# An attention layer with two layer norms, on one core: new orders for the first three rounds and the last five pairs, and the last two tiles' output bias added by TensorE

## The reference, cut to what matters

```
xn  = layernorm(x)                        # x is 8 x 2048 tokens of 512
Q,K,V = xn Wq + bq, xn Wk + bk, xn Wv + bv    # each token: 16 heads of 32
P   = softmax over k of (Q[q] . K[k]) / sqrt(32)   # per token, q and k over the 16 heads
o   = P V, laid out as (head, token, 32) and read back as (token, 512)
y   = o Wo + bo
x1  = x + layernorm(y)                    # "A": statistics of y
z   = layernorm(layernorm(x1)) * ln_g + ln_b   # "B": statistics of x1, both norms at once
out = x1 + layernorm(z)                   # "C": statistics of z
```

## Time and profile before

| | us |
|---|---|
| median of three runs | 1566.44 |
| the profiled execution | 1567.45 |
| its span, first to last instruction | 1565.7 |
| TensorE busy | 1528.8 (98%) |
| VectorE busy | 1371.3 (88%) |
| GpSimd busy | 1356.3 (87%) |
| ScalarE busy | 839.7 (54%) |

### The profile page before, as it was taken

The page is one execution under the profiler, slowest core; times in us unless marked ns, Lnnn a source line. Parts: engine busy times, 40 slices in busy tenths (PEclk is TensorE's granted clock), DMA queues, the critical chain, the costliest instruction groups (busy, mean ns, idle before and its releaser), DMA issues.

```text
span 1565.7 us, 59257 instructions
## 1 busy us (share of the span) xinstructions
PE 1528.8 (98%) x22566; PEld 773.4 (49%) x22566; DVE 1371.3 (88%) x2476; ACT 839.7 (54%) x1754; POOL 1356.3 (87%) x1422
## 2 busy tenths in 40 slices
PE   7999999999999999999999999999999999999993
PEld 3445455455554554554554554554554554554541
DVE  7788988988988988988988889888889888888888
ACT  5445465465465565555554554554554554554654
POOL 3668988988988988988988989989989989889867
PEclk9999999999999999999999999999999999999997
DMA  6776766766766766766767767767767767767652
GB/s 235 196 173 162 215 171 191 212 167 195 212 165 198 211 168 198 210 166 202 206 166 206 203 166 208 201 167 210 199 166 212 196 168 213 193 169 214 163 138 95
DMA packets 388651, 293.71 MB, mean 188 GB/s; under 512 B 296854, under 2 KB 296854, under 8 KB 388380
## 3 DMA queue, kind: packets, MB, share of 16 engines
q1 hardware_dynamic: 345936, 223.54, 53.8%
q10 hardware_dynamic: 42444, 66.37, 13.6%
HBM read 155.46 MB, written 67.24 MB: 142 GB/s over the span
## 4 chain that ended last, share of the span: by engine, by line
PE 92%; DVE 3%; POOL 2%; DMA 1%; ACT 1%; issue 1%; SPq 0%; ACTq 0%; POOLq 0%; DVEq 0%
PE ps_k L1299 7%; PE ps_q L1299 7%; PE ps_v L1299 7%; PE ps_v L1300 7%; PE ps_y L1402 7%; PE ps_q L1300 7%; PE ps_k L1300 7%; PE ps_q L1302 7%; PE ps_y L1405 7%; PE ps_y L1401 7%; PE ps_k L1302 7%; PE ps_v L1302 7%; PE ps_s L1357 6%; PE ps_o L1379 5%; DMA x_t<-in_xt 0%
## 5 line engine op out<-in xcount | busy, mean ns | idle before, releaser
L1099 ACT ACTIVATE q_sb<-ps_q,qk_back 128x512 f32<-128x512 f32 x127 | 87.2, 687 | 411.3 <-PE ps_q L1302 400.4
L474 POOL TENSOR_TENSOR o_sb<-o_sb,x 128x512 f32<-128x512 f32 x122 | 153.6, 1280 | 90.6 <-ACT o_sb L1058 90.5
L444 POOL TENSOR_TENSOR x_t<-x_t,mr_row 128x512 f32<-128x512 f32 x126 | 194.4, 1543 | 19.9 <-DMA mr_row<-x_d 10.2
L451 POOL TENSOR_TENSOR x_t<-x_t,mr_row 128x512 f32<-128x512 f32 x126 | 194.8, 1546 | 0.5
L1401 PE MATMUL ps_y<-wo_hi,oT_hi 128*128 128x512 f16 x500 | 190.5, 381 | 0.0
L1402 PE MATMUL ps_y<-wo_lo,oT_hi 128*128 128x512 f16 x500 | 190.4, 381 | 0.0
L1299 PE MATMUL ps_k<-wk_hi,xT_hi 128*128 128x512 f16 x496 | 188.6, 380 | 0.0
L1299 PE MATMUL ps_v<-wv_hi,xT_hi 128*128 128x512 f16 x496 | 188.2, 379 | 0.0
L1300 PE MATMUL ps_v<-wv_lo,xT_hi 128*128 128x512 f16 x496 | 188.2, 379 | 0.0
L1299 PE MATMUL ps_q<-wq_hi,xT_hi 128*128 128x512 f16 x496 | 188.0, 379 | 0.1
L1300 PE MATMUL ps_k<-wk_lo,xT_hi 128*128 128x512 f16 x496 | 188.0, 379 | 0.0
(11 more groups left out here) (226 smaller groups left out, 3355.1 us busy)
## 6 DMA issues: line engine op xcount, KB each, us to landing
x_in<-in_xa SPq DMA_DIRECT2D x64, 512.0 KB, 6.4
x_t<-in_xt SPq DMA_DIRECT2D x64, 512.0 KB, 8.4
k_bd<-kT SPq DMA_DIRECT2D x512, 64.0 KB, 3.3
v_d<-v_tok ACTq DMA_DIRECT2D x128, 256.0 KB, 2.5
v_key<-v_d SPq DMA_DIRECT2D x128, 256.0 KB, 4.3
res<-in_xr SPq DMA_DIRECT2D x64, 512.0 KB, 5.7
p_bd<-pT ACTq DMA_DIRECT2D x500, 64.0 KB, 2.7
out<-o_sb SPq DMA_DIRECT2D x62, 512.0 KB, 7.3
```

The costliest lines, as they stand in the source:

```text
L444: nc.gpsimd.tensor_tensor(x_t[v % 2][:, j, :, :], x_t[v % 2][:, j, :, :], mr_row[v % 2][:, :, 0, j].unsqueeze(1).to_broadcast([P, EC, P]), ...
L451: nc.gpsimd.tensor_tensor(x_t[v % 2][:, j, :, :], x_t[v % 2][:, j, :, :], mr_row[v % 2][:, :, 1, j].unsqueeze(1).to_broadcast([P, EC, P]), ...
L474: nc.gpsimd.tensor_tensor(o_sb[:, v % 2, j, :], o_sb[:, v % 2, j, :], x1[:, v % 3, j, :], ALU.add).then_inc(out_done, 1)
```

## The change

It reorders the hand-written start and end of every list, and gives the last two tiles another way to get their bias.

* Start. `spread("v")` has another bank (`ps_o`) and waits no more for the evened keys' weight. DVE makes the first `xT_lo` ahead of `scale("k")`, evens out the values' weight later, and turns the first probabilities ahead of `scale("o")`; both `low("o")` go ahead of the loop. In `project` the low-by-high products come ahead of the high-by-low ones for tiles 0 and 1. ACT issues both first `probs_half_out` ahead of `v_in(2)`. SP has `next_x(4)`, `load_r(0)`, then `values_back(0)`, `keys_out(2)`, `values_back(1)`; `rows_load(3)` now stands behind `values_back(2)` and `values_back(3)`; `load_r(1)` a round later. `spare(14)` is `spare(16)`.
* End. PE runs `mixed(124)` ahead of `scores(126)` and `output(123)` ahead of `values(127)`. The lists of DVE, ACT, POOL and SP have other orders from pair 59 on.
* Bias. DVE makes `y_fore`, the product of the two weights' scales, and `y_eps`; ACT makes `bo_fore`, the bias times `y_fore`. PE writes it into the banks of tiles 126 and 127 with a one-row f32 matmul (`bias`) behind `mixed(126)`, and `output` adds to it. DVE's `end_sums("A")` and ACT's `end_turn("A")` then read the bank itself, so `y_in(126)` and `y_in(127)` are gone; `y_eps` scales the layer norm's epsilon to match.

The core of the diff:

```diff
@@ PE
-            pe.wait_ge(w_even, 2)
             spread("v")
...
-            spare(14)
+            spare(16)
             values(1)
...
             output(NT - 6)
+            mixed(NT - 4)
             scores(NT - 2)
             scores(NT - 1)
-            mixed(NT - 4)
             mixed(NT - 3)
+            output(NT - 5)
             values(NT - 1)
-            output(NT - 5)
             output(NT - 4)
             output(NT - 3)
             mixed(NT - 2)
+            bias(END + 2)
+            bias(END + 3)
             mixed(NT - 1)
...
+            def bias(t):
+                if t == END + 2:
+                    pe.wait_ge(bo_fore_done, 1)
+                    pe.wait_ge(y_done, END)
+                else:
+                    pe.wait_ge(vtok_done, NT)
+                nc.tensor.matmul(y_bank.get(t, ps_y[:, :]), ones[:, :], bo_fore[:, :], start=True, stop=False, skip_group_check=True)
@@ SP
             keys_out(1)
+            next_x(4)
+            sp.wait_ge(w_split, 4)
+            load_r(0)
             values_back(0)
+            keys_out(2)
             values_back(1)
             rows_of(2)
-            keys_out(2)
+            next_xt(3)
             probs_half_out(0)
             probs_half_out(1)
             keys_out(3)
-            next_xt(3)
-            rows_of(3)
-            sp.wait_ge(w_split, 4)
+            rows_store(3)
...
                 values_back(b - 2)
                 if p == 2:
-                    next_x(4)
-                    load_r(0)
+                    rows_load(3)
+                if p == 3:
                     load_r(1)
@@ DVE
+            dve.wait_ge(xhi_done, 1)
+            nc.vector.tensor_tensor(xT_lo[0][:, :, :], x_t[0][:, 0, :, :], xT_hi[0][:, :, :], ALU.subtract
+                                    ).then_inc(first_low, 1)
             scale("k")
...
             less_top(NT - 4)
+            z_stat(NV - 5, 0)
             less_top(NT - 3)
             weigh(NT - 4)
+            weigh(NT - 3)
+            z_stat(NV - 5, 1)
+            p_turn(NT - 4)
+            moments("C", NV - 5)
             k_turn(NT - 2)
-            p_turn(NT - 4)
-            z_stats(NV - 5)
-            weigh(NT - 3)
             x1_stats(NV - 4)
+            o_low(NT - 6)
+            p_turn(NT - 3)
+            o_low(NT - 5)
+            out_add(NV - 5, 0)
+            k_turn(NT - 1)
             q_turn(NT - 2)
-            out_add(NV - 5, 0)
+            z_add(NV - 4, 0)
+            q_turn(NT - 1)
...
             end_z_lean(END)
+            end_sums("A", END + 3)
             end_z_out(END)
-            end_sums("C", END)
-            y_in(END + 2)
-            end_sums("A", END + 2)
-            y_in(END + 3)
@@ ACT
             probs_half_out(0)
+            probs_half_out(1)
             v_in(2)
-            probs_half_out(1)
+            cast("o", 0, wo_hi)
             q_in(3)
+            cast("o", 1, wo_hi)
             x_high(4)
@@ POOL
             out_add(NV - 3, 0)
             out_add(NV - 3, 1)
+            end_root_of("B", END + 3, 1.0 + EPS, EPS * EPS)
+            end_out_add(END)
+            end_out_add(END + 1)
             end_root_of("C", END + 2)
```

More of the change, by code:

```diff
@@ L63, in fused @@
         y_back = sb("y_back", [P, 1])
+        y_fore = sb("y_fore", [P, 1])
+        y_eps = sb("y_eps", [P, 1])
+        bo_fore = sb("bo_fore", [1, E])
         x_in = [sb(f"x_in{i}", [P, 2, E]) for i in range(2)]
@@ L397, in _ @@
             values_back(NT - 3)
+            store(NV - 6)
+            keys_out(NT - 2)
+            probs_half_out(NT - 4)
+            keys_out(NT - 1)
+            probs_half_out(NT - 3)
             sp.wait_ge(x1_done, 2 * (NV - 4))
             load_r(NV - 3)
-            store(NV - 6)
-            keys_out(NT - 2)
+            values_back(NT - 2)
+            store(NV - 5)
+            store(NV - 4)
             sp.wait_ge(x1_done, 2 * (NV - 3))
             load_r(NV - 2)
[L404 to L409, removed]
             probs_half_out(NT - 2)
@@ L414, in _ @@
             load_r(NV - 1)
+            store(NV - 3)
+            end_store(END)
             end_store(END + 1)
-            end_store(END)
-            store(NV - 3)
             end_store(END + 2)
@@ L913, in _ @@
             low("v", 0, wv_hi, wv_lo)
+            low("v", 1, wv_hi, wv_lo)
             k_turn(1)
-            low("v", 1, wv_hi, wv_lo)
             q_turn(1)
@@ L920, in _ @@
             less_top(1)
+            weigh(0)
+            weigh(1)
+            p_turn(0)
+            q_turn(2)
+            p_turn(1)
+            k_turn(3)
             scale("o")
             product_scale(y_back, "v", "o", 1.0, y_scale_done)
[L923 to L928, removed]
             x_moments(3)
             q_turn(3)
+            low("o", 0, wo_hi, wo_lo)
+            low("o", 1, wo_hi, wo_lo)
             for p in range(2, NV - 1):
@@ L963, in _ @@
                     z_scale(v)
+            dve.wait_ge(w_scaled, 8)
+            nc.vector.scalar_tensor_tensor(y_fore[:, :], scale_of("v"), 1.0, scale_of("o"), ALU.mult, ALU.mult).then_inc(y_fore_done, 1)
+            dve.wait_ge(y_fore_done, 1)
+            nc.vector.scalar_tensor_tensor(y_eps[:, :], y_fore[:, :], EPS, y_fore[:, :], ALU.mult, ALU.mult).then_inc(y_fore_done, 1)
             y_in(NT - 7)
@@ L967, in _ @@
             less_top(NT - 4)
+            z_stat(NV - 5, 0)
             less_top(NT - 3)
             weigh(NT - 4)
+            weigh(NT - 3)
+            z_stat(NV - 5, 1)
+            p_turn(NT - 4)
+            moments("C", NV - 5)
             k_turn(NT - 2)
-            p_turn(NT - 4)
-            z_stats(NV - 5)
-            weigh(NT - 3)
             x1_stats(NV - 4)
-            q_turn(NT - 2)
-            out_add(NV - 5, 0)
-            out_add(NV - 5, 1)
[L978 to L985, removed]
+            o_low(NT - 6)
[3 more added lines that the diff above has]
+            k_turn(NT - 1)
+            q_turn(NT - 2)
+            z_add(NV - 4, 0)
+            q_turn(NT - 1)
+            z_stat(NV - 4, 0)
+            z_add(NV - 4, 1)
+            z_stat(NV - 4, 1)
+            out_add(NV - 5, 1)
+            moments("C", NV - 4)
+            y_in(NT - 6)
             less_top(NT - 2)
-            y_in(NT - 6)
+            less_top(NT - 1)
             y_stats(NT - 6)
-            less_top(NT - 1)
             weigh(NT - 2)
             o_low(END)
-            o_low(END + 1)
+            y_in(NT - 5)
             p_turn(NT - 2)
-            y_in(NT - 5)
             y_stats(NT - 5)
@@ L997, in _ @@
             y_in(END)
+            o_low(END + 1)
+            p_turn(NT - 1)
             end_sums("A", END)
-            p_turn(NT - 1)
             end_moments("A", END)
@@ L1173, in end_turn @@
                 act.wait_ge(end_shift[i], turn)
+                if k == "A" and t >= END + 2:
+                    act.wait_ge(y_ready, t + 1)
+                    act.wait_ge(out_done, 2 * (t // 2 - 3) + t % 2 + 1)
                 if k == "C" and t < END + 2:
@@ L1253, in _ @@
                 x_high(b + 2)
+            act.wait_ge(b_loaded, 3 * DMA)
+            act.wait_ge(y_fore_done, 1)
+            nc.scalar.activation(bo_fore[:, :], bo_row[0:1, :], ACT.Copy, scale=y_fore[0:1, 0:1]).then_inc(bo_fore_done, 1)
             o_high(NT - 6)
```

127 lines of the change are left out of this document (65 added, 62 removed).

## The result

The changed kernel took 1571.68 us (median of six runs, 1570.17 to 1574.16), the kernel before 1567.03 in six runs beside it (1565.5 to 1568.93). The ratio is 1.0029, with an interval of 1.0019 to 1.0039: slower, by 4.5 us, where 7.3 us faster were forecast. The profiled execution took 1570.17 us, the least of the six, and spans 1568.4 (before: 1567.45 and 1565.7).

What follows compares the result with a forecast made beforehand. TensorE, busy 1179.95 of 1180 us in the loop, was taken as the bound, leaving only start and end to win. Start 2.7, end 3.1 and behind the last matmul 1.5 made 7.3: 1566.44 to 1559.1 us, range 1555.5 to 1563.8.

Steps and rivals of the forecast that it cites:

- Start, up to the third tile: From the kernel's start to keys(2): reordered lists bring it 1.75 us sooner, between 0.6 and 3.8.
- Start, to the loop: From keys(2) to the loop: the 1.0 us p_bd wait goes, start total 2.7 us; a later rows_load(3) is made up.
- rival 3: In the loop: shifted instruction supply leaves TensorE gaps each round; at 0.2 us a round 1571.3 us; chance 0.06.
- Loop: The steady rounds between start and end: same instructions, so nothing won or lost.
- End, first wait: TensorE's wait for q_turn(127), 2.06 us before: becomes 1.3 us for p_bd of tile 125, clock staying up.
- End, second wait: Ahead of mixed(127), 2.04 us before: start near 1534, gap filled by 2.1 us of bias products keeping full clock.
- rival 2: At the end: the clock falls all the same after a p_bd wait near 2 us; 1561.3 us; chance 0.12.
- Behind the last matmul: From TensorE's last product to VectorE's last instruction, 19.5 us before: 1.5 us won, between -1 and 3.
- Rival 1: In the start: rows_load(3) behind values_back(3) delays GpSimd and keys_out(5), giving the gain back; 1561.8 us; chance 0.13.

Runs made afterwards that it cites:

- S: The changed kernel with only SyncE's start put back as in the kernel before; 1565.4 us, ratio 0.9981 to the kernel before.
- v127_first: S with values(127) put back ahead of output(123) on TensorE; 1563.7 us, ratio 0.9976 to the kernel before.
- no_bias: S without the two one-row bias products of the last two tiles; 1565.5 us, ratio 0.9981 to the kernel before.
- filler: S with eight full 128x512 16-bit products, later overwritten, between the two bias products; 1564.4 us, ratio 0.9978 to the kernel before.
- loads_back: The changed kernel with next_x(4) and load_r(0) moved back behind rows_load(3); 1570.0 us, ratio 1.001 to the kernel before.
- start_only: The kernel before with the change's start in all lists and the old end; 1571.3 us, ratio 1.0019 to the kernel before.
- rows_back: loads_back with rows_of(3), store and load, also put back ahead of the loop; 1566.5 us, ratio 0.9989 to the kernel before.
- v127_turn: v127_first with VectorE's p_turn(127) ahead of y_in(124) and o_low(125); 1566.0 us, ratio 0.9988 to the kernel before.
- v127_tail: v127_first with end_out_add(124) moved to VectorE and GpSimd's root A of tile 127 ahead of root C of 125; 1564.0 us, ratio 0.9973.

## Why the prediction was wrong

The sum was 2.7 (start) + 3.1 (end) + 1.5 (behind) = 7.3. What the runs give for the same terms: 2.5 for the start without SyncE's list, about 0.5 (inside the intervals) for end and tail together, and -7.5 for SyncE's list, which the sum had at nothing: -4.5.

* *Start, up to the third tile* (1.75). Right in mechanism, too low: `xT_lo` took 0.69 instead of 1.65, and `queries(0)` waited 0.59 for `low("q")` (0.8 forecast). `keys(2)` came 3.1 us sooner, near the upper end of 3.8.
```profile
12.13 0.69 DVE L914 TENSOR_TENSOR xT_lo<-x_t,xT_hi 128x512 f16<-128x512 f32 x1
```
 The Trainium skill ("SBUF — State Buffer", SBUF: two separate sides) says that a VectorE instruction with two SBUF inputs and a GpSimd instruction that reads SBUF shut each other out of a shared pair of ports for their whole length. This case agrees: 1.65 us beside a GpSimd subtraction that had started 0.46 us sooner and ran until 1.10 us into it, 0.69 with GpSimd idle.
* *Start, to the loop* (0.95 more, and what is late next). **This step failed**, at the words "In favour: ... 1.5 MB of loads leave the stretch ahead of this DMA, two for earlier". I took the place that the loads left as a gain and never asked what stands at the place they went to. There the first `v_d` store was due 0.4 us behind them, and SyncE's own next entry waits for it. A moved DMA has to be counted at its new place too; this one wasn't: 3.0 us. The second part of the step, `rows_load(3)`, named the right chain (`x_centre(6)`, `normalise`, `keys_out(5)`, `k_bd`) and sized it at 1.4 us covered by lighter traffic; it cost 3.3 and was covered by nothing. I reckoned its issue at 60, which doesn't follow from my own row: 65.03 less 2.7 is 62.3, so that `x_centre(6)` would have come at 66.4, a microsecond later than before and 3.7 behind TensorE instead of 1.4. It came at 64.87 and landed after 6.24. A third load put ahead of the halves of `p_bd` may be part of the remaining 1.3, which no run shows clear of noise. What is right in the step is that the 1.0 us wait for `p_bd` goes once SyncE's start is undone (S).
* *Loop*: right, and rival 3 with it is refuted (1179.96 of 1180 us).
* *End, first wait* (1.3 us for `p_bd`, clock up): right, 0.19 and 0.93 with clock 1.00 (the 1518.7 of the working is 0.2 short of its own terms, which changes nothing); `keys(127)` didn't wait for `k_turn(126)`.
* *End, second wait*: the size of the bias was right (0.96 us each; 1.03 taken), and so was its cover. Wrong was that `p_bd` would be the late one and `mixed(127)` start at 1534, which with the shift of the start is 1537.1. It came at 1538.88, for `v_key`: `values(127)` had gone behind `output(123)`, 2.6 us of TensorE, and I costed that move at nothing; with it undone, in v127_first, the wait is gone. Wrong as well was that the bias keeps TensorE at 2.4 GHz (no_bias, filler). So rival 2, the falling clock, held, by another wait than it named.
* *Behind the last matmul* (18 us): it was 19.5, as before. The two `y_in` went, but the chain that ended last runs through GpSimd's list from 1545.17 to its last root, with 1.57 us of idle time for tile 126 ahead of it, and root A of tile 127 came no sooner behind TensorE than before (6.9 and 7.2). I had counted the two orders as even. No run undoes this order alone, so how much it costs isn't shown.

Rivals 1 and 2 both happened. Rival 1 was to give back 2.7 at most; its mechanism alone cost 3.3 and the loads 3.0. No rival had a transfer slowed by another that was moved beside it.

## What to carry to other kernels

A load has a price at its new place: look for the store or the small DMA on the critical chain that is issued within its landing time, on any queue, and for what SyncE holds behind the wait. A queue entry that waits for a store holds up everything behind it, here `keys_out(2)`, the row that the next tiles need and `p_bd`; look at what that is before moving it. At the end, an order is judged by what each wait ends on next, and a gain on TensorE counts only as far as the engine that finishes the work can use it.

## What the runs showed of the hardware

* The first 256 KB store to DRAM landed in 2.0 to 2.1 us in the kernel before, S and loads_back, and in 5.6 and 6.2 (changed, start_only) behind two loads of 512 KB issued up to 1.1 us earlier on another engine's queue. SyncE's transfers of `p_bd`, 64 KB each, took medians of 2.3 (before) and 2.7 us (S) with no such load right ahead of them, and 5.4 (changed), 6.1 (rows_back) and 6.5 (loads_back) right behind one.
* TensorE's clock, in one execution each: 2.3 us of idle time in v127_turn, amid full products, were followed by 1.00; two one-row f32 products and then 1.73 us of idle time by 0.59; the same two with no idle time before `mixed(127)` by 1.00 in v127_first's profile and by 0.78 and 0.50 in v127_tail's.
* A one-row f32 product of 1x512 took 0.96 us at full clock, a little over the prediction's estimate of 0.85.
